# One attention and expert block on one core: transposes, weight loads and gathers in another queue order, and the last block's queries and keys projected before the sums of the block before

## What is computed

```python
q = jnp.einsum('bpm,hmd->bphd', x, Q_w) + Q_b
k = jnp.einsum('bpm,hmd->bphd', x, K_w) + K_b
v = jnp.einsum('bpm,hmd->bphd', x, V_w) + V_b
logits = jnp.einsum('bqhd,bkhd->bhqk', q, k) / math.sqrt(d_head)
logits = jnp.where(causal_mask, NEG, logits)
scores = jax.nn.softmax(logits, axis=-1)
attn = jnp.einsum('bhqk,bkhd->bqhd', scores, v)
out = jnp.einsum('bqhd,hdm->bqm', attn, O_w) + O_b
...
x = x + ga * attention(h)
h = _layernorm(x, axis=-1) * (1 + cb) + sb
x = x + gb * ffn(h)
```

## Time and profile before

| | us |
|---|---|
| three timed executions | 2114.26, 2116.16 (median), 2117.55 |
| the profiled execution, its own time | 2118.04 |
| its span (first to last instruction) | 2116.2 |
| PE busy | 2006.9, 95% of the span |
| DVE, ACT, POOL busy | 1394.5, 1103.7, 382.9 |
| mean granted clock of PE | 0.986 of full speed |

### The profile page before, as it was taken

One profiled execution on the slowest core, in us unless ns is written; L12 is line 12 of the kernel. 1 busy time (PEld: TensorE's weight loads), 2 busy tenths in 40 slices (PEclk: granted clock), 3 DMA queues, 4 the chain that ended last, 5 costly groups with the idle time before them and its releaser, 6 DMA issues.

```text
span 2116.2 us, 33069 instructions
## 1 busy us (share of the span) xinstructions
PE 2006.9 (95%) x9863; PEld 1503.0 (71%) x9865; DVE 1394.5 (66%) x3219; ACT 1103.7 (52%) x1638; POOL 382.9 (18%) x393
## 2 busy tenths in 40 slices
PE   6899999999999999999999999899999999999978
PEld 3677766777667677767776676667887778777767
DVE  7687676786686767866867877656554853333367
ACT  4476666675675756656756757542334134444311
POOL 5211010110110110101101101434000222222364
PEclk9999999999999999999999999999999999999999
DMA  6488787788878877877888788896432079999665
GB/s 214 85 161 161 155 163 158 155 168 161 168 154 161 170 157 149 169 159 153 166 159 168 155 168 166 183 199 190 146 100 66 1 227 296 318 302 317 212 189 169
DMA packets 932173, 366.06 MB, mean 173 GB/s; under 512 B 754800, under 2 KB 885920, under 8 KB 932128
## 3 DMA queue, kind: packets, MB, share of 16 engines
q1 hardware_dynamic: 921888, 331.93, 69.6%
q0 software_dynamic: 10240, 33.56, 5.1%
HBM read 138.86 MB, written 41.94 MB: 85 GB/s over the span
## 4 chain that ended last, share of the span: by engine, by line
PE 60%; SPq 11%; DVE 10%; DMA 6%; issue 5%; ACT 5%; POOL 2%; another core or an unknown queue 1%; DVEq 0%; ACTq 0%; POOLq 0%
SPq L472 8%; PE gen L1572 8%; PE gen L1574 8%; PE gen L1573 8%; PE strip L1572 5%; PE strip L1574 5%; PE strip L1573 5%; PE strip L1868 5%; PE pv L1572 4%; PE pv L1574 4%; PE pv L1573 4%; DMA pT<-p_lo 2%; PE strip L1875 2%; ACT p_hi L861 2%; ACT exps L852 2%
## 5 line engine op out<-in xcount | busy, mean ns | idle before, releaser
L1179 DVE SCALAR_TENSOR_TENSOR p_lo<-exps,rinv,p_hi 128x512 f16<-128x512 f32 (+3 forms) x256 | 390.9, 1553 | 64.3 <-ACT p_hi L861 63.7
L852 ACT ACTIVATE exps<-exps,nbias 128x128 f32<-128x128 f32 (+15 forms) x256 | 306.9, 1200 | 164.0 <-DVE nbias L1165 164.0
L861 ACT ACTIVATE p_hi<-exps,rinv 128x512 f16<-128x512 f32 (+3 forms) x256 | 334.7, 1353 | 86.9 <-DMA pT<-p_lo 55.6
L1155 DVE TENSOR_SCALAR_CACHE_REDUCE exps<-strip 128x512 f32<-128x512 f32 x384 | 253.1, 687 | 150.6 <-PE strip L1574 148.2
L1572 PE MATMUL strip<-kT_hi,qT_hi 128*128 128x512 f32 (+3 forms) x640 | 241.2, 377 | 43.6 <-DVE kT_lo L1127 37.3
L1573 PE MATMUL strip<-kT_lo,qT_hi 128*128 128x512 f32 (+3 forms) x640 | 237.8, 372 | 0.0
L1574 PE MATMUL strip<-kT_hi,qT_lo 128*128 128x512 f32 (+3 forms) x640 | 237.6, 371 | 0.0
L1572 PE MATMUL pv<-pT,v 128*128 128x512 f16 (+3 forms) x640 | 223.1, 349 | 7.8 <-DMA pT<-p_lo 7.8
L709 POOL TENSOR_TENSOR wq_lo<-wq_raw,wq_hi 128x512 fp32r<-128x512 f32 x16 | 20.6, 1291 | 1117.8 <-ACT wq_hi L831 1117.8
L1573 PE MATMUL pv<-pT,v 128*128 128x512 f16 (+3 forms) x640 | 222.6, 348 | 0.0
L1574 PE MATMUL pv<-pT,v 128*128 128x512 f16 (+3 forms) x640 | 219.5, 348 | 0.0
(11 more groups left out here) (236 smaller groups left out, 4289.8 us busy)
## 6 DMA issues: line engine op xcount, KB each, us to landing
at_dram<-at_f SPq DMA_DIRECT2D x64, 256.0 KB, 2.6
wg_sb<-in_L_ffn_Wg SPq DMA_DIRECT2D x64, 256.0 KB
wu_sb<-in_L_ffn_Wu SPq DMA_DIRECT2D x64, 256.0 KB
wd_sb<-in_L_ffn_Wd SPq DMA_DIRECT2D x64, 256.0 KB
yb_dram<-yb SPq DMA_DIRECT2D x64, 256.0 KB
a_f<-at_dram SPq DMA_DIRECT2D x58, 256.0 KB, 2.9
pT<-p_hi SPq DMA_TRANSPOSE x320, 3.4
pT<-p_lo SPq DMA_TRANSPOSE x320, 3.3
```

The source lines that it names most:

```text
L852: nc.scalar.activation(row, row, ACT.Exp, bias=nbias[:, t:t + 1], accum_out=rsum[:, t:t + 1]).then_inc(row_probs, 1)
L861: nc.scalar.activation(p_hi16[:, 0:j + 1, t, :], row, ACT.Copy, scale=rinv[:, t:t + 1]).then_inc(p_hi, 1)
L1155: nc.vector.tensor_scalar(exps[:, t, 512 * ch:512 * ch + w], strip[u % STRIPS][:, 0:w], SCALE, None, ALU.mult, ALU.max, accum_out=cmax[:, ...
L1179: nc.vector.scalar_tensor_tensor(p_lo16[:, 0:j + 1, t, :], row, rinv[:, t:t + 1], p_hi16[:, 0:j + 1, t, :], ALU.mult, ALU.subtract).then_i ...
```

## The change

1. **PE, ACT, DVE, stage 2.** `AHEAD = (0, 2)` names the stages in which the next block's queries and keys come straight behind the scores: stage 0 as before, and now stage 2 as well. On PE they go ahead of the sums of block 1. On ACT `gen_hi_of("q")` and `("k")` go behind the fourth exponential, ahead of `probs_hi` of row tiles 2 and 3. On DVE `gen_out_of("q")` and `("k")` go behind the last `row_inverse`, ahead of `probs_lo` of tiles 2 and 3.
2. **SP, stage 1.** The values of block 1 are transposed between the `_hi` and the `_lo` transposes of the first rows, no longer ahead of both; the next head's weights are loaded behind the last rows of stage 1, no longer at the head of the loop.
3. **SP, last head.** The first six loads of output weights go together behind the transposes of stage 1; before, three went ahead of them and three between first and last rows.
4. **Gathers.** Each gather has its own semaphore. POOL now waits before every gather for the one three before it; DVE waits for each gather by itself.

```diff
-        GATHS = 4
+        GATHS, GATHERS_OUT = 4, 3
...
+        AHEAD = (0, 2)
...
@@ SP
                 for g in range(j + 1):
                     wait_alone(pv_group, slot_free(groups_before(j) + g, h))
                     turn_pair(h, j, 0, g, 0)
+                if j == 1:
+                    turn_values(h, 1, h)
                 wait_alone(p_lo, h * NT + (TB * j + 2))
...
                 turn_first_rows(h, j)
                 turn_last_rows(h, j)
+                if j == 1:
+                    load_weights(h)
                 if prev is not None:
                     store_at(*prev)
-                if nxt is not None and nxt[1] > 0:
+                if nxt is not None and nxt[1] > 1:
                     turn_values(*nxt, nxt[0])
...
             with sp.Fori(0, H - 1) as h:
-                load_weights(h)
...
-            for hd in range(0, 3):
-                load_wo(hd)
-            turn_first_rows(H - 1, 1)
-            for hd in range(3, 6):
-                load_wo(hd)
-            turn_last_rows(H - 1, 1)
+            turn_first_rows(H - 1, 1)
+            turn_last_rows(H - 1, 1)
+            for hd in range(6):
+                load_wo(hd)
             store_at(H - 1, 0)
...
@@ POOL
                 for k in range(TOPK):
-                    if k == TOPK // 2 and t >= 1:
-                        pool.wait_ge(g_landed[(t - 1) % GATHS], 16 * TOPK * ((t - 1) // GATHS + 1))
+                    n = t * TOPK + k - GATHERS_OUT
+                    if n >= 0:
+                        pool.wait_ge(g_landed[n // TOPK % GATHS][n % TOPK], 16 * (n // (TOPK * GATHS) + 1))
...
@@ ACT
                     exp_row(h, j, 2)
                     exp_row(h, j, 3)
+                    if j in AHEAD:
+                        gen_hi_of("q", nxt[1], nxt[0])
+                        gen_hi_of("k", nxt[1], nxt[0])
                     probs_hi(h, j, prev, 2)
                     probs_hi(h, j, prev, 3)
...
@@ DVE
                     probs_lo(h, j, 1)
                     row_inverse(h, j, 3)
+                    if j in AHEAD:
+                        gen_out_of("q", nxt[1], nxt[0])
+                        gen_out_of("k", nxt[1], nxt[0])
                 probs_lo(h, j, 2)
                 probs_lo(h, j, 3)
...
                     for k in range(TOPK):
+                        dve.wait_ge(g_landed[t % GATHS][k], (t // GATHS + 1) * 16)
...
@@ PE
                 score(h, j)
-                if j == 0:
+                if j in AHEAD:
                     project("q", *reversed(nxt))
                     project("k", *reversed(nxt))
                 if prev is not None:
                     ...
                     sum_values(hp, jp)
                 if nxt is not None:
                     hn, jn = nxt
-                    if j > 0:
+                    if j not in AHEAD:
                         project("q", jn, hn)
                         project("k", jn, hn)
```

More of the change, by code:

```diff
@@ L320, in adaln_block @@
         yb_stored = [sem(f"yb_stored{i}") for i in range(EX)]
-        g_landed = [sem(f"g_landed{i}") for i in range(GATHS)]
+        g_landed = [[sem(f"g_landed{i}_{k}") for k in range(TOPK)] for i in range(GATHS)]
         gath_free, combined = sem("gath_free"), sem("combined")
@@ L810, in _ @@
                         in_offset=bass.IndirectOffsetOnAxis(ap=slot_u[:, t, k:k + 1], axis=0)
-                    ).then_inc(g_landed[t % GATHS], 16)
+                    ).then_inc(g_landed[t % GATHS][k], 16)
         @block.scalar
@@ L903, in stage @@
                     attended(*prev)
-                if j == 0:
-                    take_at_scale(h)
+                if j in AHEAD:
+                    if j == 0:
+                        take_at_scale(h)
                     gen_hi_of("v", nxt[1], nxt[0])
@@ L1554, in combine_beside @@
                 for t in COMBINE[step]:
-                    dve.wait_ge(g_landed[t % GATHS], (t // GATHS + 1) * 16 * TOPK)
                     for k in range(TOPK):
+                        dve.wait_ge(g_landed[t % GATHS][k], (t // GATHS + 1) * 16)
                         link(nc.vector.scalar_tensor_tensor(acc[:, t, :], gath[t % GATHS][:, k, :], w_top[:, t, k:k + 1],
```

## The result

The changed kernel takes 2107.19 us, the median of 7 runs (2106.03 to 2110.93), beside 2115.04 for the kernel before on the same chip (2110.43 to 2117.55). The ratio is 0.997, with a 95% interval of 0.9958 to 0.9982: a little faster. The forecast was 2106.8. The profiled execution took 2110.93, span 2109.1, where the kernel before had 2118.04 and 2116.2.

What follows compares the result with a forecast made beforehand. PE, busy 95%, was taken as bound, its gaps set by a chain through SP, DMA, ACT and DVE. 2118.04 - 13.2 (loop) + 2.0 (head 0) + 1.9 (last head) = 2108.7 profiled, so 2106.8 median; range 2097 to 2119.

Steps and rivals of the forecast that it cites:

- SP's order frees 4.3 us: SP, stage 1: probabilities go out ahead of values and weight loads, so block 2's `p_hi` starts at 269.5, not 273.79.
- The slot takes most of it back: SP, stage 2: group 2's transpose waits from 275.5 to 279.0 for block 1's moved sum; about 1 of 4.3 is left.
- Rival A: SP finds the slot free, PE is the bound at 79.9 a head, 2073 in all; chance 0.10.
- Rival C: The chain behind the slot is 1 us a head longer, so nothing measurable changes, 2117 to 2121; chance 0.14.
- The new cycle of 81.8: Closed chain of one head through SP, ACT, DVE and PE: 81.8, with about 1.9 of PE waiting ahead of score(0).
- the four drops: Granted clock in the loop: four drops of 1.4 in fourteen heads stay, 0.4 a head, making 82.2 against 83.14.
- Rival B: PE's waits ahead of score(0) and the output projection let the clock drop, ten more heads pay 1.4: 2123; chance 0.10.
- Head 0, 2.0 lost: Start of the loop, old chain not yet closed: score(0) comes at 148.4 instead of 146.43, 2.0 lost once.
- The last head, 1.9 lost: SP's bunched output weight loads wait for POOL's splits, delaying block 3's `p_hi` and the output projection by 1.9; bounds 0 and 6.
- Gathers 0: Waiting for the gather three before costs 0, DVE's last sums lying well behind the last gather; bounds 0 and 3.

Runs made afterwards that it cites:

- e1: The changed kernel with block 3's queries and keys put behind the sums of block 1 again: 2083.17 us, 0.983 of the kernel before.
- e4: The changed kernel with low halves of groups 0 and 1 sent ahead of the transpose that waits for the slot: 2081.63 us, 0.9813 of the kernel before.
- e9: The kernel before with SP's stage 1 order, new gathers and five useless DVE reductions ahead of block 3's low keys: 2100.91 us, ratio 0.9932.
- e3: The changed kernel with the first six loads of output weights back in their old places in the last head: 2094.22 us, 0.9883 of the kernel before.
- e7: The kernel before with the new waits of the gathers alone: 2114.32 us, ratio 1.0005.
- e11: The kernel before with only the values' transpose moved behind the first two of the probabilities in SP's stage 1: 2062.43 us, ratio 0.9753.
- e5: The kernel before with SP's new order in stage 1 and the new gathers, nothing else: 2068.28 us, ratio 0.9785.
- e10: The kernel before with SP's stage 1 order, new gathers and seven useless DVE reductions ahead of block 3's low keys: 2132.53 us, ratio 1.0085.

## Why the forecast came out right

The total agrees, 2107.19 beside 2106.8, and that is partly luck. Two of its terms were off, by 7.2 (the loop won more) and 9.2 (the last head lost more), with opposite signs; head 0 lost 1.8 less than forecast and the part behind the output projection took 2.0 more. Together that leaves the profiled execution 2.2 above its forecast of 2108.7, and the median lies 3.7 below that execution, not 1.9. The mechanism of the loop held: SP's earlier transposes win time, and the slot takes most of it back.

- **SP's order frees 4.3 us.** It does: ACT starts block 2's copies at 269.30, forecast 269.5. The cover named for the moved weight loads held: they stand at 267.7 to 269.2.
- **The slot takes most of it back.** Forecast a wait of 3.5, measured 3.0 (2.8 to 3.1 in the loop), and shown to be the cause by e1 and e4. Rival A, the case without this wait, is what these two kernels are: 79.8 a head, where 79.9 was worked out. Rival C, a chain 1 us longer, did not come either.
- **The new cycle of 81.8.** Measured 81.68. The place of PE's remaining wait was missed: not `kT_lo` ahead of score(0) for 1.9, but mostly `at_f` ahead of the value bound (1.0 to 1.3), and 0.2 for `kT_lo`. As I read the order of work, both come from ACT being late by the same chain, so the length was right and the place wrong. The two waits make 1.2 to 1.5 a head; the rest of what lies above 79.8 shows as PE's busy time (80.4), and no run says why.
- **What 81.8 was compared with.** This step failed. 83.14 is a mean over nine heads of 82.47 and five of 84.35, so the chain gained only 0.79 a head; and the four drops that I kept as a cost of the new kernel did not come. I priced a drop by PE's busy time alone, 1.4 (81.48 less 80.08 in the earlier trace rows); no run shows a head longer by that, and by the distance of the heads it is 1.88. The loop was forecast at 13.2 and gave 20.4. The reason given for keeping them, that the wait that stays is nearly as long as the one that goes, overlooked that it would be split: 1.0 to 1.3 and 0.2, both shorter than the 1.89 at which no head of e9 fell. Rival B, built on the same thought, is answered by e9: waits of 1.89 in each head cost about their own length (2.1) and no drop.
- **Head 0, 2.0 lost.** From the end of score(2) to score(0) it takes 39.8 (146.62 - 106.84) where it took 38.1 (146.43 - 108.36): 1.7 lost, near the 2.0 forecast. It doesn't show in the total because score(2) ended 1.5 earlier in this execution; over the runs its end lies between 106.3 and 109.1, with either order.
- **The last head, 1.9 lost.** The mis-sized term. The mechanism was right, loads in front of block 2's transposes waiting for POOL's splits, and so was the place of stage 1 (nine transposes ending 38.6 behind score(0), forecast 38.4). But SP came to block 2 61.6 behind score(0), forecast 53.3. A split was put at 1.9; but the first ended 8.5 behind its load (1328.79 to 1337.3), forecast 5.65 as in the earlier trace rows, and the six ends lie 13.9 apart (1337.3 to 1351.2), forecast 5 x 1.9 = 9.5; four of the casts and subtractions took 2.15 to 2.69 instead of 0.6 and 1.3, beside DVE's `p_lo`. That is 7.3 of the 8.3. The upper bound of 6 was too low as well: the loss is 11.1 beside the old last head and 13.0 beside e3's.
- **Gathers 0.** Confirmed by e7.

What the runs leave open: why the heads that fall are five and not others at the same wait, how much of the last head's loss is the slow splits and how much the order alone, and whether e11 is really faster than e5.

## What to carry to other kernels

When an in-order queue carries work for several consumers, look first for the one item that waits longest at its head: here one transpose of values ahead of the probabilities was worth 2.5%, and the rest of the change gave most of that back through a buffer slot freed later and loads bunched in front of the last head's transposes. A mean over periods hides two populations; take the distances one by one before comparing a chain's length with them. And where a queue waits on another engine's buffer, try moving independent items into that wait: the low halves cost nothing there (e4, 79.80 a head, PE's own pace).

## What the runs showed of the hardware

- **Longer waits of PE, more heads at the lower clock.** Each count is from one profiled execution of fourteen heads; the lower level is a granted clock of 0.50 for 3.41 us. 1.89 us in each head: 0 of 14 at the lower level; 2.3 to 2.5: 5 of 14, in two kernels; 3.07: 9 of 14. The first and the last are the same loop but for two reductions. The edge isn't sharp at 1.89: in the last head of e7 a wait of 1.99 was followed by the lower level. A fallen head is 1.6 (e10) to 1.9 us (before) longer than one of the same loop that did not fall.
- **POOL's splits take longer beside DVE's `p_lo`.** A cast of 0.61 became 2.15, and a subtraction of 1.30 became 2.67, and each of the four long ones of the changed kernel's last head starts while a `p_lo` runs and ends about its own usual length behind the end of that `p_lo`; with none running (1347 to 1353) they are 0.60 to 0.61 and 1.26 to 1.28. One subtraction, at 1341.24, stayed at 1.30 though a `p_lo` had begun 0.02 before it; there it was the `p_lo` that took 2.93 instead of its usual 1.81. In the fourteen traces 49 such subtractions start while a `p_lo` runs, and 48 of them take 2.1 to 3.4. That is a coincidence in time in the traces, not an experiment. The trace of the kernel before has it in its own last head: two casts of 2.14 and a subtraction of 2.65 start while a `p_lo` runs (at 1362.31, 1365.76 and 1367.98). Weighed before the forecast, they would have put some of the splits at 3.4 (the first of them, 2.14 and 1.30) or more, and the term nearer to its size.
